# First attention: the mask of the one-head score banks moves from TensorE to VectorE's maximum, and the reciprocal of the sums stays in PSUM

## What is computed

```python
scores = jnp.einsum('bhqd,bhkd->bhqk', q, k_h) / math.sqrt(HEAD_DIM)
causal = jnp.triu(jnp.ones((t, t), dtype=bool), k=1)
scores = jnp.where(causal[None, None], jnp.finfo(scores.dtype).min, scores)
attn = jax.nn.softmax(scores, axis=-1)
ctx = jnp.einsum('bhqk,bhkd->bhqd', attn, v_h)
```

## Time and profile before

| | |
|---|---|
| Median of 3 runs | 1460.55 us (1460.55 to 1463.03) |
| The profiled execution | 1460.84 us |
| Its span, first to last instruction | 1459.0 us |
| Mean granted TensorE clock | 0.985 |
| First TensorE instruction of attend0 / of feed_forward0 | 71.5 / 377.9 us |
| Busy: PE, DVE, ACT, POOL | 93%, 70%, 50%, 47% of the span |
| Key copies (L1393) start at | 74.5, 109.0, 138.3, 167.8, 197.4, 227.0, 266.3, 305.8 us |

### The profile page before, as it was taken

How to read it: one execution, slowest core, us unless ns; L and a number is a source line. 1 busy time by engine, 2 the same in 40 slices (tenths; PEclk the granted TensorE clock), 3 DMA queues, 4 the chain that set the end, 5 groups by cost and what they waited for, 6 DMA issues and landing times. The chain is left out here.

```text
span 1459.0 us, 20197 instructions
## 1 busy us (share of the span) xinstructions
PE 1359.1 (93%) x6904; PEld 1086.5 (74%) x6904; DVE 1020.4 (70%) x2063; ACT 726.4 (50%) x1574; POOL 685.4 (47%) x533
## 2 busy tenths in 40 slices
PE   4779999988898699999999999999999999699999
PEld 3656666655576588888888888888888887578887
DVE  6769998785757677778777787778877878532322
ACT  2548887676534355444544454545544454243332
POOL 3548887666363544244433543444424431055453
PEclk9989999999999999999999999999999999999999
DMA  3000000100110211011110110101101010043332
GB/s 108 3 28 1 1 1 1 25 6 15 52 36 1 73 30 44 9 36 30 29 38 8 37 37 16 44 15 30 44 15 30 22 44 1 15 107 83 103 93 82
DMA packets 64933, 50.72 MB, mean 35 GB/s; under 512 B 5760, under 2 KB 54272, under 8 KB 64576
## 3 DMA queue, kind: packets, MB, share of 16 engines
q1 hardware_dynamic: 64832, 49.43, 11.9%
HBM read 47.32 MB, written 2.10 MB: 34 GB/s over the span
## 5 line engine op out<-in xcount | busy, mean ns | idle before, releaser
L1683 POOL TENSOR_TENSOR a_p_lo<-a_prob,a_p_hi 128x512 fp32r<-128x512 f32 x160 | 203.8, 1288 | 86.3 <-ACT a_p_hi L1573 84.4
L695 ACT ACTIVATE a_pt_hi<-a_ring 128x512 fp32r<-128x512 f32 x160 | 93.8, 596 | 175.8 <-PE a_ring L402 175.7
L831 POOL TENSOR_TENSOR a_rot_a<-a_rot_a,a_rot_b 128x512 f32<-128x512 f32 x80 | 103.5, 1294 | 139.1 <-DVE a_rot_b L574 139.1
L686 ACT ACTIVATE a_prob<-a_score,a_nmax 128x128 f32<-128x128 f32 (+3 forms) x256 | 132.0, 529 | 57.4 <-DVE a_nmax L539 29.0
L2296 POOL TENSOR_TENSOR f_w_lo<-raw,f_w_hi 128x512 fp32r<-128x512 f32 (+2 forms) x66 | 90.8, 1402 | 142.4 <-ACT f_w_hi L2239 142.3
L340 PE MATMUL a_xo<-h_hi,a_w_hi 128*128 128x512 f32 x384 | 151.2, 394 | 5.3 <-POOL a_w_lo L841 4.2
L342 PE MATMUL a_xo<-h_hi,a_w_lo 128*128 128x512 f32 x384 | 151.1, 393 | 0.0
L341 PE MATMUL a_xo<-h_lo,a_w_hi 128*128 128x512 f32 x384 | 150.4, 392 | 0.0
L836 POOL TENSOR_TENSOR a_p_lo<-a_rot_a,a_p_hi 128x512 fp32r<-128x512 f32 x80 | 103.3, 1292 | 69.4 <-ACT a_p_hi L712 69.4
L556 DVE TENSOR_TENSOR a_pt_lo<-a_ring,a_pt_hi 128x512 fp32r<-128x512 f32 x160 | 108.5, 686 | 33.1 <-ACT a_pt_hi L695 32.1
L1573 ACT ACTIVATE a_p_hi<-a_prob 128x512 fp32r<-128x512 f32 x160 | 99.7, 629 | 45.0 <-PE a_cbank L1203 43.0
(11 more groups left out here) (330 smaller groups left out, 3763.8 us busy)
## 6 DMA issues: line engine op xcount, KB each, us to landing
raw<-in_L_gate_up_t SPq DMA_DIRECT2D x40, 256.0 KB, 3.0
raw<-in_L_attn_wq SPq DMA_DIRECT2D x32, 256.0 KB, 2.8
raw<-in_L_attn_wo SPq DMA_DIRECT2D x32, 256.0 KB, 2.7
raw<-in_L_down_t SPq DMA_DIRECT2D x20, 256.0 KB, 2.7
x<-in_L_attn_x SPq DMA_DIRECT2D x4, 512.0 KB, 5.6
raw<-in_L_attn_wk SPq DMA_DIRECT2D x8, 256.0 KB, 2.8
raw<-in_L_attn_wv SPq DMA_DIRECT2D x8, 256.0 KB, 2.8
out<-x SPq DMA_DIRECT2D x8, 256.0 KB, 2.5
```

Of the source, the lines that this page charges most:

```text
L686: nc.scalar.activation(prob[i % 2][:, h, 0:n], score[e % NS][:, (h % per) * n:(h % per + 1) * n], ACT.Exp, bias=nmax[:, i % 2, h:h + 1], s ...
L695: nc.scalar.activation(pt_hi[:, n % NPT, :], ring[n % 2][:, :], ACT.Copy).then_inc(pt_hi_done, 1)
L831: nc.gpsimd.tensor_tensor(rot_a[:, c % 2, :], rot_a[:, c % 2, :], rot_b[:, c % 2, :], ALU.add).then_inc(summed, 1)
L1683: nc.gpsimd.tensor_tensor(p_lo[:, mm % NP, :], prob[:, mm % NE, :], p_hi[:, mm % NP, :].bitcast(F32), ALU.subtract).then_inc(p_ready, 1)
```

## The change

For banks of one head (i = 2 and 3) TensorE leaves out the mask matmul, and VectorE takes the maximum with `masked_maximum`, which adds the mask as it reads and writes the masked scores back. Banks of two and four heads stay as they are, and so do the transposed scores. In `take_heads` the reciprocal is written over the sums in hbank, and the multiplication reads it there; rsum is gone. `turn_back` therefore waits for the multiplication of the block before (`head_ready`), not for its add.

```diff
-        rsum, head_sum = sb("rsum", [P, 2, HPG, X2]), sb("head_sum", [P, HPG, X2, HD0])
+        head_sum = sb("head_sum", [P, HPG, X2, HD0])
...
                 out = claim_score()
+                scored_by[QT * u + i] = count["score"]
+                if per == 1:
+                    nc.tensor.matmul(out[:, 0:n], q_rows[:, bank, :], k_rows[:, u % 2, x, 0:n], start=True,
+                                     stop=True).then_inc(scored, 1)
+                    return
...
                 if n >= 1:
-                    pe.wait_ge(divided, 3 * n)
+                    pe.wait_ge(head_ready, n)
...
                 per, n = HPG // S_BANKS[i], (i + 1) * P
+                if per == 1:
+                    if u == 0 and i == 2:
+                        dve.wait_ge(zeroed, 3)
+                    masked_maximum(nc, m, next_score(), n, nmax[:, i % 2, bank, x:x + 1]).then_inc(score_read, 1)
+                    return
...
-                s, r = head_sum[:, :, :, :], rsum[:, n % 2, :, :]
+                s, r = head_sum[:, :, :, :], view[:, :, :, HD0]
                 dve.wait_ge(backed, n + 1)
-                nc.vector.reciprocal(r, view[:, :, :, HD0]).then_inc(divided, 1)
+                nc.vector.reciprocal(r, r).then_inc(divided, 1)
```

More of the change, by code:

```diff
@@ L1174, in scores @@
                                  start=False, stop=True).then_inc(scored, 1)
-                scored_by[QT * u + i] = count["score"]
             def turned_scores(u, i, x, j):
```

## The result

| | before | changed |
|---|---|---|
| Median of the runs | 1463.26 us (1460.55 to 1465.73, 12 runs) | 1456.74 us (1453.78 to 1459.62, 12 runs) |
| Ratio to before, 95% interval | | 0.9952 [0.9942, 0.9961] |
| The profiled execution, its span | 1460.84, 1459.0 us | 1456.81, 1454.9 us |
| Granted clock | 0.985 | 0.982 |

The change is worth 0.48%, some 7 us. The forecast was 11.6 us (0.8%). The sign and the range held, the range by 0.3 us at its upper end (1457); the size did not. The forecast started from a median of 1460.55 us in three runs; twelve runs of the same kernel give 1463.26.

The account below looks back on a forecast made before the run. TensorE was taken to bound units 1 to 4 of attend0, VectorE and GpSimd close behind. Gains 6.8 + 3.4 + 1.0 + 0.4 = 11.6 us from 1460.84 gave 1449.2, as median 1449.0 us; range 1444 to 1457.

Parts of the forecast that it names:

- units 5 and 6: In attend0, these two units were each to gain 1.7 us like units 1 to 4, 3.4 us together.
- the sum for units 1 to 4: In attend0, TensorE needs 27.1, VectorE 26.7, GpSimd 25.7 us; period taken as 27.8, gaining 1.7 a unit, 6.8 us.
- Part 1, TensorE: In attend0, 128 mask matmuls go at 0.13 us each: 2.1 us a unit, 16.6 us in all as upper end.
- Part 2, the masked maximum: On VectorE, 128 reductions become two instructions each, 0.05 us dearer apiece, 0.8 us a unit.
- Part 3, the division: On VectorE, the last multiplication reads the reciprocal from hbank and costs 0.36 us less each, 1.4 us a unit.
- the wait of `turn_back`: It moves from the add to the multiplication behind it, at no cost; uncovered, 0.3 us for each of 31.
- The reciprocal, taken as unchanged: In the division, it writes to PSUM instead of SBUF; no change taken, between none and 0.29 us.
- Rival 1: The small subtraction L1383 is held by GpSimd in its three other instances a unit too: 1456.5 us, chance 0.18.
- The mask nearly free: On TensorE, dropping the masks saves only 0.6 us a unit (0.04 us a mask): 1456.0 us, chance 0.05.
- VectorE the bound: Unhidden accumulator reads cost 0.16 us a maximum and VectorE sets the pace: slower, 1473.7 us; slower had chance 0.05.
- The clock: New waits bring two or three half-clock stretches of TensorE, 4 us go back: 1453 us, chance 0.05.
- half clock between 100 and 300 us: Listed sign that the forecast is wrong: TensorE at half clock in that part of the trace.

Follow-up runs that it names:

- second looks: The kernel before and the changed kernel, both unchanged, each profiled a second time: spans 1464.0 and 1457.4 us.
- the split free: Against the changed kernel, put_maxima makes its high and low parts with three one-source reductions instead of a cast and a subtraction: 1448.31 us.
- division and split: Against the kernel before, the reciprocal in PSUM and put_maxima made of three reductions, masks left on TensorE: 1455.13 us.
- the split: Against the kernel before, only put_maxima's cast and subtraction replaced by three reductions: 1463.18 us, ratio 1.0001.

## Why the prediction was right in sign and wrong in size

Beside the sum of the prediction, what the two pairs of profiles gained from unit 0's key copy to feed_forward0, in us:

| | forecast | first looks | second looks |
|---|---|---|---|
| unit 1 | 1.7 | -1.5 | 0.9 |
| units 2 to 4 | 5.1 | 1.3 | 1.3 |
| units 5 and 6 | 3.4 | 3.6 | 3.5 |
| unit 7 | 1.0 | 0.7 | 1.8 |
| unit 0 | 0.4 | -0.1 | -0.4 |
| sum | 11.6 | 4.0 | 7.1 |

Units 2 to 6 ran at full clock in all four profiles and agree: 4.8 to 4.9 us gained where 8.5 were forecast. Units 0, 1 and 7 have stretches of half clock of different length in the two kernels of a pair, so their rows don't tell the change from the clock. In unit 7 they are equally long in the first pair (6.8 us), and it gained 0.7.

That units 5 and 6 came out at the forecast is luck. It gave them the 1.7 of the other units, most of it for the masks; by the experiments the division brings 1.3 to 1.4 of it and the masks 0.4 to 0.5 (37.87 to 37.41 us in unit 5 with the split free).

**The step that failed** is the sum for units 1 to 4: a period of 27.8 us from three engines' needs. It took each engine's need as the period less its waits, for VectorE 27.3 + 0.8 - 1.4 = 26.7 us, and asked only whether an engine has room in a unit. That need came out near (29.2 less the 2.1 us of its waits in unit 2 is 27.1, of which 0.8 is the held cast). It did not ask whether the two instructions between the last maximum and `turn_queries(.., 1)` come in time. TensorE waited 0.3 us there, so there was nothing to spare at this place: each us by which VectorE came later, or TensorE earlier, became a wait. The masks saved TensorE 1.3 us, and 1.2 us went into this wait (0.3 to 1.5). Counted against what TensorE needs when nothing else binds, 28.7 and 27.4 us, the periods of 29.6 and 29.1 lie 0.9 and 1.8 above it: the need fell by 1.3, the loss grew by 0.9, and 0.4 was left. The prediction asked after a hold only for instructions with two SBUF inputs, L1383 and L1432; the cast, with one, it passed over, and freeing the cast alone gives 1.2 of the 1.8 us back.

**Part 1, TensorE.** The saving is 0.08 us a mask where nothing else binds, not 0.13; the pair of 155.15 is one of the places that do save 0.13, and most save 0.04 to 0.05. The need with masks was 28.7, not 29.2 us. The 29.2 was TensorE's period less its visible waits; division and split shorten the unit to 28.7 without taking a matmul from TensorE. The two errors nearly cancel by luck: 29.2 - 2.1 = 27.1 was forecast as the floor, 27.4 is measured.

**Part 2, the masked maximum.** Right: 0.52 us (182.56 to 183.08) and 0.65 us (185.21 to 185.86) where I had written 0.50 and 0.63.

**Part 3, the division.** Right in price (286 ns for 726 in the median) and in the wait of `turn_back`, which appears nowhere. Its effect was undervalued: it was to help the mask's saving along, and alone it brought 5.4 of the 6.5 us. The reciprocal, taken as unchanged, takes 0.01 us more (median 207 ns before, 216 now), and the copy behind it grew more than that (below).

**Rival 1** (the small subtraction held in its other three instances, because the gaps of GpSimd close; 1456.5 us) gave nearly the measured time, by half its mechanism. The gap that closes is there. But the three other subtractions stayed short (the four of unit 2 take 1.72 us together, as in the earlier trace rows), and the cast in front of the fourth was caught. The argument against it, that the order of weighing and scores stays, was about the order alone; the hole of 0.42 us at 193 us was smaller than the shift. It was to be read before: the earlier trace rows show the subtraction starting just 0.13 us after GpSimd's row of 163.81 began, so the cast 0.2 us ahead of it had got through in the hole.

**The other rivals.** The mask nearly free: true in most places, but 0.08 us in the mean lies halfway, and would alone have cost 0.8 us a unit of the forecast's limit, hidden here by the wait. VectorE the bound: no, it has 2.4 us to spare a unit. The clock: half clock between 100 and 300 us was a sign of being wrong and came true (108 us), but the kernel before has it as well (110.6 us), and the runs of both kernels have the same mean clock.

## What to carry to other kernels

A saving on the busiest engine is lost at the first place where that engine already waits a little for another; look for the waits of 0.3 us and ask what stands in front of them, rather than for room in the sum of an engine. On VectorE, a tiny instruction in such a place wants a form that GpSimd didn't hold here: a reduction over an axis of length 1 does the work of a cast, and one over two columns, one stored negated, that of a subtraction. Freeing one instruction can hand the hold to the next that can be held, as the split did on the kernel before. Try the parts of a change in all combinations before judging one of them: here the same edit was worth -1.6, 1.1, 5.7 or 6.8 us.

## What was not expected of the hardware

A cast of 128x8 numbers from SBUF to SBUF can wait for GpSimd as an instruction with two sources does, up to 1.17 us behind GpSimd's subtractions, and 0.39 us behind a fill of 0.52 us. One held instruction of eight numbers lost 6.14 us at a stretch. And the copy of hbank behind the reciprocal has grown, though it is the same instruction (before, then changed; count, busy us, mean ns):

```profile
L1425 DVE COPY a_head_sum<-a_hbank 128x128 f32<-128x128 f32 x32 | 7.6, 238 | 0.0
...
L1434 DVE COPY a_head_sum<-a_hbank 128x128 f32<-128x128 f32 x32 | 8.9, 278 | 0.2
```

40 ns more each, 1.3 us of VectorE's time in all. It comes with the division's part of the change: the mean is 277 to 279 ns in all seven profiles with the reciprocal in hbank and 238 to 239 in all five with rsum, wherever the masks are and whatever the split. In that part the reciprocal ahead of the copy now writes into the bank that the copy reads, and `turn_back` waits for another instruction; which of the two it is wasn't tried. Nor was it tried why the subtraction passed four chances before it got in.
